# A gated delta-rule attention block: outputs and gates turned to time on the partitions

## The chip, the cores and the metric

The kernel runs on one core of one Trainium2 chip. The metric is device time of one execution in microseconds, lower is better. Times of a kernel are medians of several executions.

## What is computed

Three blocks in a row on an input of 4 x 512 tokens by 512: a feed-forward block whose weights are splines of control points, an attention block, and the feed-forward block again. The change touches the attention block alone. There, for each of 16 key heads (two value heads each) and each of 4 sequences:

```python
q, k, v, z = split(x @ W_qkvz)            # z gates the output
q, k, v = silu(causal_conv4(q, k, v))
q, k = rms_norm(q) / D, rms_norm(k) / sqrt(D)
S = S * exp(g_t)                          # per token t, per value head
delta = (v_t - k_t @ S) * beta_t
S = S + outer(k_t, delta)
o_t = q_t @ S
out = silu(z) * (rms_norm(o) * norm_w)    # norm over the 128 columns of a head
y += out @ W_out                          # sum over all heads
```

## The kernel before

**Phases.** The spline weights and the first feed-forward block take the start, then a norm phase, then `attn_phase`, then the second feed-forward block. `attn_phase` works through 64 units: a unit is one key head with its R = 2 value heads, for one sequence of S = 512 tokens, cut in CH = 4 chunks of P = 128. Unit j belongs to key head j // 4. Five engine programs (`pe_pass`, `act_pass`, `dve_pass`, `pool_pass`, `sp_pass`) are written out by hand in one order each, and wait for one another by counted semaphores. In slot j an engine handles the recurrence of unit j (`has_delta`), prepares unit j + 1 (`has_prep`: projections, convolutions, norms, the decay matrices), and finishes the output of unit j - 1 (`behind`).

**The inverse.** The first part of a slot inverts a 512-token set of unit-triangular 128 x 128 blocks by doubling, in level steps s = 2 to 13; step s works on value head g = s % 2. PE issues prod (four f16 matmuls into `psP`), DVE masks the result into `pm` (L2033), PE issues inv (eight f16 matmuls, L1657 and L1659, into `psT[g]`), ScalarE copies it out (`copy_t`, L1850). Steps 0 and 1 are `level_0` of either head; that of head 1 stands at the end of the slot before. Other work is hung on the steps: on PE `fill[s]` stands between prod(s) and inv(s); on DVE `steps[s]` stands behind the mask of step s and ahead of the mask of step s + 1; on ScalarE `steps[s]` stands behind the copy of inv(s).

**The chunks.** Then four chunks of the recurrence follow, with the rest of the projections in `gap`, and at the end `s_o` says that both heads' outputs are in PSUM, in `psO` (banks that `psT[1]` and `psP` use as well). POOL's copy of `dcy` (L2147) waits for `s_o` of the unit before and so opens the next slot.

**The output.** Values stand with the 128 columns of a head on the partitions and time along the free side. `squares` (ScalarE) squares `psO` into `osq`, DVE multiplies `psO` by `norm_w` and the silu of z (L2074, `d_gate`), `gated` rounds it to `gt_hi`, POOL takes the rest as `gt_lo` (`low_outputs`). `out_sums` on PE turns the squares into sums per token by 8 f32 matmuls of one column (16 passes), `out_scale` on POOL makes the factor `fr`. `out_product(i)` multiplies one head's chunk by `wo_hi`, `wo_lo` (three f32r matmuls of 512 columns into `out_bank`, which is `psM`), and `out_add` (L2007) multiplies by `fr` and adds into `resid`: eight products and eight additions a unit, in steps 5 to 12. The projection of z is 24 matmuls of 512 columns, with W as the stationary side. POOL also splits the weights of the next key head (`split_part`, `split_wo`) and masks the gates (`mask_g`).

Of the kernel before, what the change touches and what calls it, by code (L numbers as in the profile page):

```python
# [30 lines left out]
P = 128  # L31
# [4 lines left out]
D = 128  # L36
# [1221 lines left out]
WPROD = R * CH  # L1258
# [3 lines left out]
def attn_phase(nc, w_qkvz, conv_w, norm_w, w_out, cst_in, cst16_in, resid, x_hi, x_lo, gate_dram, decay_dram, y_dram):  # L1262
# [7 lines left out]
    with ExitStack() as ctx:  # L1270
# [3 lines left out]
        def sem(name):  # L1274
# [20 lines left out]
        cv_z = sb("cv_z", [P, R, S])  # L1295
# [158 lines left out]
        def pe_pass(pe):  # L1454
# [5 lines left out]
            for j, has_delta, has_prep, behind, ends in slots():  # L1460
                par = j % 2

                def bank_free(u, j):
# [5 lines left out]
                    if u == Z0_U:  # L1469
                        wait(pe, "d_conv", 4 * j + 1 if has_prep else 4 * j - 1)  # L1470
                        wait(pe, "d_sso", j)
# [30 lines left out]
                def out_product(i, of):  # L1502

                    h, c = i // CH, i % CH
                    wait(pe, "p_gt", R * of + h + 1)
                    if of % B == 0:
                        wait(pe, "p_wo", R * (of // B + 1))
                    if i > 0:
                        wait(pe, "d_y", WPROD * of + i)
                    else:  # L1510
                        wait(pe, "d_aqk", R * (j + 1))
                    out = out_bank[:]
                    mm(out, ch(gt_hi[:, h], c), wo_hi[:, h, :], True, False)
                    mm(out, ch(gt_hi[:, h], c), wo_lo[:, h, :], False, False)
                    own["s_w"].up(mm(out, ch(gt_lo[:, h], c), wo_hi[:, h, :], False, True))
# [52 lines left out]
                def out_sums(of):  # L1568

                    wait(pe, "a_sqo", R * (of + 1))  # L1570
                    if of == UNITS - 1:
                        wait(pe, "d_z", 2 * UNITS)
                    else:
                        wait(pe, "d_conv", 4 * j + 1 if has_prep else 4 * j - 1)
                    for i in range(R * CH):
                        last = mm(psA[0][:, i:i + 1], ch(osq[:, i // CH], i % CH), ones[:, 0:1])
                    own["s_sso"].up(last)

# [17 lines left out]
                gap = {g: [] for g in range(3 * CH)}  # L1596
                if behind:
                    fill[2].append(lambda: out_sums(j - 1))
                if has_prep:
                    fill[3].append(parts(Q_U, 7, 12))  # L1600
                if has_delta:
                    fill[4].append(parts(Z0_U, 0, 5))
                    fill[5].append(parts(Z0_U, 5, 6))
                    fill[6].append(parts(Z0_U, 7, 8))
                    fill[7].append(parts(Z0_U, 9, 10))
                    for k in range(5):
                        fill[8 + k].append(parts(Z1_U, 2 * k, 2 * k + 1))
                if behind:
                    for i in range(WPROD):
                        fill[5 + i].append(lambda i=i: out_product(i, j - 1))  # L1610
                if has_delta:
                    fill[5].append(parts(Z0_U, 6, 7))
                    fill[6].append(parts(Z0_U, 8, 9))
                    fill[7].append(parts(Z0_U, 10, 12))
                    for k in range(5):
                        fill[8 + k].append(parts(Z1_U, 2 * k + 1, 2 * k + 2))
                    fill[13].append(parts(Z1_U, 10, 12))
                if has_prep:
                    fill[13].append(turn_k)
# [87 lines left out]
                for c in range(CH):  # L1707
                    if has_delta:
# [3 lines left out]
                        else:  # L1712
# [6 lines left out]
                            for h in range(R):  # L1719
                                mm(ch(psO[h], c), state[:, h, :], ch(qg[:, h], c - 1), True, False)  # L1720
# [11 lines left out]
                    if has_delta:  # L1732
# [6 lines left out]
                        for h in range(R):  # L1739
                            last = mm(ch(psO[h], c), delta[:, h, :], ch(aqk[:, h], c), c == 0, True)  # L1740
# [10 lines left out]
                if ends:  # L1751
                    out_sums(j)
                    for i in range(WPROD):
                        out_product(i, j)
# [3 lines left out]
        def act_pass(act):  # L1758
            own = counters("a_")
            A = nc.scalar.activation  # L1760
            for j, has_delta, has_prep, behind, ends in slots():
# [90 lines left out]
                def squares(h):  # L1852
                    wait(act, "s_o", j + 1)
                    if h < R - 1:
# [11 lines left out]
                if behind:  # L1866
                    steps[2].append(lambda: gated(j - 1, 1))
                if has_prep:
                    steps[3].append(lambda: tap(Q_U))
                    steps[4].append(lambda: tanh(K_U))  # L1870
                    steps[7].append(lambda: tanh(Q_U))
                if has_delta:
                    steps[8].append(lambda: tanh_z(Z0_U))
                if has_prep:
                    steps[13].append(square_k)
# [47 lines left out]
                if has_delta:  # L1923
                    for h in reversed(range(R)):
                        squares(h)
                    gated(j, 0)
# [3 lines left out]
                if ends:  # L1930
                    gated(j, 1)
            finish(act, own)

        def dve_pass(dve):
# [8 lines left out]
            for j, has_delta, has_prep, behind, ends in slots():  # L1943
# [21 lines left out]
                def silu_z(u):  # L1965
                    wait(dve, "a_thz", 2 * j + u - 3)
                    wait(dve, "p_gt", R * j)
# [24 lines left out]
                def out_sums(i):  # L1992

                    wait(dve, "s_sso", i + 1)
# [364 lines left out]
```

How the kernel before makes its waits and increments, by code:

```python
            @block.gpsimd  # L380
            def _(pool):
                nc.gpsimd.memset(f32(st_g[:]), 0.0).then_inc(zeroed, 1)
                nc.gpsimd.memset(f32(st_b[:]), 0.0).then_inc(zeroed, 1)
                pool.dma_start(wts[:, 0:2 * GSUM], gsum_in).then_inc(sums_in, 16)
                pool.dma_start(groups(wts, S_FD, 4 * P), dsum_in.rearrange("p (g n) -> p g n", g=4)).then_inc(sums_in, 16)
                for u in range(UNITS + 4):
                    pool.wait_ge(hi_done, u + 1)
                    nc.gpsimd.tensor_tensor(weights(u, False), quarters(merged[:, u % 2, :]), f32(weights(u, True)), ALU.subtract).then_inc(lo_done, 1)
                pool.wait_ge(lo_done, UNITS + 4)
                pool.wait_ge(sums_in, 32)
# [1 line left out]
            @block.vector  # L392
# [4 lines left out]
                def chain(ins):  # L397
                    count[0] += 1
                    ins.then_inc(link, 1)
                    dve.wait_ge(link, count[0])
# [24 lines left out]
                    V.tensor_scalar(d3, c3, 0.5 * step ** 3, None, ALU.mult)  # L425
                    chain(V.tensor_scalar(d1, c1, 0.5 * step, None, ALU.mult))
                    if reach:
                        chain(V.scalar_tensor_tensor(d1, d3, float(reach), d1, ALU.mult, ALU.add))
                dve.wait_ge(tap_g_in, 32)
                cubics(tap_g, phi_g, d_g, NG, 0)
                dve.wait_ge(zeroed, 1)
# [30 lines left out]
                for u in range(UNITS + 4):  # L463
                    if u == 0:
                        dve.wait_ge(eval_in, 32)
                    if u == UNITS:
```

## Time and profile before

| | us |
|---|---|
| median of 3 runs (3988.17 to 3993.54) | 3991.61 |
| the profiled execution | 3988.65 |
| its span, first to last instruction | 3986.9 |
| PE matmul busy / weight loads busy | 3711.7 (93%) / 2984.8 (75%) |
| DVE / ScalarE (ACT) / POOL busy | 2447.1 (61%) / 1986.3 (50%) / 2344.9 (59%) |
| mean granted TensorE clock | 0.963 of 2.4 GHz |

Matmuls are pipelined: a duration reaches beyond the start of the next, so the distance between starts tells what one costs. A row of the timeline is start in us, duration in us, engine, line, operation, output <- inputs, shape, count; in brackets the idle time of the engine before it and what ended it. The f32 matmuls appear as two passes each. Units are counted from 0; unit j is the slot that POOL's copy of `dcy` opens for the (j + 1)th time.

### The profile page before, as it was taken

To read this page: it belongs to the slowest core of one execution; us is meant where nothing else is said; L and a number is where in the kernel's file an instruction comes from. 1 tells how busy PE (TensorE), PEld (TensorE's weight loads), DVE (VectorE), ACT (ScalarE), POOL (GpSimd) and SP (SyncE) were. 2 spreads that over 40 slices of the span, in tenths; PEclk is the share of its full clock that TensorE was granted. 3 is DMA by queue.
4 is the path that set the end of the run, shared out by engine and by line. 5 is a ranking of instruction groups with operands and counts; after the bars stand their busy time and mean duration, and the time that the engine had idled before them with its cause. 6 is when DMAs were issued, how large, how long until landed. Compare 5 with 4: busy or idle time off the path is not lost. (4 is left out here: it accounts for less than half of the span.)

```text
span 3986.9 us, 74528 instructions
## 1 busy us (share of the span) xinstructions
PE 3711.7 (93%) x28324; PEld 2984.8 (75%) x28324; DVE 2447.1 (61%) x4347; ACT 1986.3 (50%) x4272; POOL 2344.9 (59%) x2805
## 2 busy tenths in 40 slices
PE   5995699999999999999999999999999999998798
PEld 4884477777777777777777777777777777776587
DVE  4654366666666666666666666666666666664464
ACT  3432355555555555555555555555555555553243
POOL 2102567676766666676676767676767676763110
PEclk8997799999999999999999999999999999998899
DMA  4333100000000000000000000000000000001521
GB/s 165 97 33 67 50 22 23 23 23 22 23 22 23 22 23 22 23 22 23 22 23 22 23 23 23 22 23 22 23 22 23 19 22 22 25 16 36 175 54 33
DMA packets 142384, 140.32 MB, mean 35 GB/s; under 512 B 84176, under 2 KB 115152, under 8 KB 140880
## 3 DMA queue, kind: packets, MB, share of 16 engines
q1 hardware_dynamic: 136992, 120.16, 10.6%
q0 software_dynamic: 4464, 14.36, 1.0%
q8 instruction: 230, 3.77, 0.4%
q14 instruction: 122, 1.00, 0.1%
q10 hardware_dynamic: 576, 1.03, 0.1%
HBM read 109.11 MB, written 26.21 MB: 34 GB/s over the span
## 5 line engine op out<-in xcount | busy, mean ns | idle before, releaser
L1850 ACT ACTIVATE at_t<-at_inv 128x512 f16<-128x512 f32 x768 | 459.0, 598 | 783.0 <-PE at_inv L1659 783.0
L1458 PE MATMUL at_proj<-x_hi,at_w_hi 128*128 128x512 f32 x1536 | 669.4, 436 | 15.7 <-POOL at_w_lo L2103 15.7
L1458 PE MATMUL at_proj<-x_lo,at_w_hi 128*128 128x512 f32 x1536 | 663.4, 432 | 0.0
L1458 PE MATMUL at_proj<-x_hi,at_w_lo 128*128 128x512 f32 x1536 | 651.9, 424 | 0.0
L2033 DVE TENSOR_TENSOR at_pm<-at_prod,at_cst 128x512 f16<-128x512 f32 x768 | 529.6, 690 | 158.3 <-PE at_prod L1458 143.7
L2007 DVE SCALAR_TENSOR_TENSOR resid<-at_misc,at_fr,resid 128x512 f32<-128x512 f32 x512 | 383.3, 749 | 137.3 <-PE at_misc L1458 134.1
L1458 PE MATMUL at_prod<-at_t,at_nlhi 128*128 128x128 f16 x3584 | 377.5, 223 | 0.9 <-DVE at_pm L2040 0.9
L1657 PEld LDWEIGHTS at_inv<-at_pm,at_t 128*128 128x128 f16 x3072 | 214.0, 101 | 218.7 <-DVE at_pm L2033 139.0
L1458 PEld LDWEIGHTS at_proj<-x_hi,at_w_hi 128*128 128x128 f32 x1536 | 299.5, 195 | 55.3 <-issue 15.9
L1458 PEld LDWEIGHTS at_proj<-x_hi,at_w_lo 128*128 128x128 f32 x1536 | 301.8, 196 | 43.1
L1458 PEld LDWEIGHTS at_proj<-x_lo,at_w_hi 128*128 128x128 f32 x1536 | 303.6, 198 | 34.0
L1657 PE MATMUL at_inv<-at_pm,at_t 128*128 128x64 f16 x3072 | 298.6, 198 | 11.4 <-DVE at_pm L2033 3.8
L2181 POOL TENSOR_TENSOR at_gt_lo<-at_cst,at_gates 128x512 fp32r<-128x512 f32 x256 | 261.9, 1045 | 77.0 <-PE at_misc L1458 77.0
L1954 DVE SCALAR_TENSOR_TENSOR at_cv_v<-at_proj,at_cw,at_cv_v 128x511 f32<-128x511 f32 (+2 forms) x384 | 287.5, 749 | 15.5 <-ACT at_cv_v L1776 2.0
L1659 PE MATMUL at_inv<-at_t,at_pm 128*128 128x64 f16 x3072 | 292.1, 196 | 0.0
L1458 PEld LDWEIGHTS at_prod<-at_t,at_nlhi 128*128 128x128 f16 x3584 | 240.6, 100 | 19.5 <-issue 18.5
L2054 DVE SCALAR_TENSOR_TENSOR at_t<-at_t,at_dcy,at_inv 128x128 f32<-128x128 f32 x256 | 77.6, 345 | 286.1 <-PE at_inv L1458 277.8
L889 PE MATMUL f_ring<-f_x_hi,ffn_w 128*128 128x512 f32 x640 | 247.2, 401 | 3.9 <-DVE f_x_lo L815 2.9
L1899 ACT ACTIVATE at_t<-at_inv 128x256 f32<-128x256 f32 x256 | 98.5, 385 | 303.5 <-PE at_inv L1716 273.5
L1910 ACT ACTIVATE at_t<-at_inv,at_gates 128x128 f32<-128x128 f32 x512 | 160.0, 364 | 175.3 <-PE at_inv L1458 175.3
L1458 PE MATMUL at_misc<-at_wo_hi,at_gt_hi 128*128 128x512 f32 x512 | 232.3, 454 | 10.5 <-DVE resid L2007 9.1
L1659 PEld LDWEIGHTS at_inv<-at_t,at_pm 128*128 128x128 f16 x3072 | 218.6, 100 | 0.0
(282 smaller groups left out, 9512.3 us busy)
## 6 DMA issues: line engine op xcount, KB each, us to landing
at_gb<-decays SPq DMA_DIRECT2D x64, 512.0 KB, 3.7
at_e<-w_qkvz SPq DMA_DIRECT2D x32, 512.0 KB, 3.7
ffn_weights<-ffn_w SPq DMA_DIRECT2D x1, 11776.0 KB, 36.8
ffn_w<-ffn_weights POOLq DMA_DIRECT2D x4, 2688.0 KB, 23.5
at_gb<-w_qkvz SPq DMA_DIRECT2D x16, 512.0 KB, 3.6
at_gb<-w_out SPq DMA_DIRECT2D x16, 512.0 KB, 3.5
f_xnext<-x_in SPq DMA_DIRECT2D x4, 1024.0 KB, 5.2
f_xres<-x_res SPq DMA_DIRECT2D x4, 1024.0 KB, 5.2
```

What stands on the lines that cost most here:

```text
L889: return nc.tensor.matmul(out, lhsT, rhs, start=start, stop=stop)
L1458: return nc.tensor.matmul(out, lhsT, rhs, start=start, stop=stop)
L1657: nc.tensor.matmul(half_of(ch(psT[g], c), level, 0), ch(t16[:, g, 1], c), half_of(ch(pm[:, g], c), level, 0), start=False, stop=True, skip ...
L1659: last = nc.tensor.matmul(half_of(ch(psT[g], CH + c), level, 1), ch(pm[:, g], c), half_of(ch(t16[:, g, 1], c), level, 1), start=False, sto ...
L1850: own["a_t"].up(A(grown(t16[:, s % R].rearrange("p a t -> p (a t)"), s // R), grown(psT[s % R], s // R), ACT.Copy))
L1899: own["a_v"].up(A(vp, psV, ACT.Copy))
L1910: own["a_d"].up(A(delta[:, h, :], ch(psY, h), ACT.Copy, scale=gcur[:, 2, at + c, h:h + 1]))
L1954: ins = V.scalar_tensor_tensor(out[:, s:S], unit_bank[u][:, 0:S - s], cw[(j + 1) // B % 2][:, u, 3 - s:4 - s], out[:, s:S], ALU.mult, ALU.add)
L2007: own["d_y"].up(V.scalar_tensor_tensor(row, out_bank[:], fr[:, h, c:c + 1], row, ALU.mult, ALU.add))
L2033: own["d_p"].up(V.tensor_tensor(pm[:, g].rearrange("p (c t) -> p c t", c=CH), psP[:].rearrange("p (c t) -> p c t", c=CH), mask.unsqueeze(1 ...
L2054: ins = V.scalar_tensor_tensor(state[:, h, :], state[:, h, :], dcy[:, h, c:c + 1], ch(psU, h), ALU.mult, ALU.add)
L2181: last = G.tensor_tensor(gm[:, k], incl.unsqueeze(1).to_broadcast([P, CH, P]), new_gates[:, g, at:at + CH, h:h + 1].to_broadcast([P, CH, P ...
```

## The change

The outputs are held with time on the partitions. The operands of the `psO` products are swapped, so that `psO` is tokens by columns. z is projected with x as the stationary side and both heads' 256 columns of W moving (`gate_part`, 48 f32r matmuls a unit). ScalarE's squares add up per token by themselves (`accum_out`, four of 128 columns a head), and `out_sums` is gone from PE and DVE. POOL makes the factor first and multiplies the gated outputs by it (`scale_gated`); then PE turns them by transposes (`turn_gated`), ScalarE rounds them out of PSUM (`gated`), DVE takes the rest (`low`), and `out_product(c)` adds both heads of a chunk in one accumulator: six matmuls each, four products and four plain additions. `norm_w` goes into W_out. Some tasks stand in other steps: taps of K's convolution on DVE are spread, `turn_k` and `square_k` come a step earlier, POOL's splits of weights move behind `mask_g(1)`.

```diff
-WPROD = R * CH
+WPROD = CH
@@ pe_pass
+                def gate_part(u, first, end):
...
+                        last = mm(unit_bank[u][:, c * R * D:(c + 1) * R * D], xs[:, hb, tok:tok + P], w[:, hb, 4 * D:6 * D],
+                                  k % (3 * HB) == 0, k % (3 * HB) == 3 * HB - 1)
+                def turn_gated(h, of):
+                    wait(pe, "p_gt", R * of + h + 1)
+                    if h == 0:
+                        wait(pe, "d_aqk", R * (j + 1))
+                    else:
+                        wait(pe, "d_lo", R * of + h)
+                    for c in range(CH):
+                        last = nc.tensor.transpose(ch(psM, c), gated_of(h)[:, c, :], ident)
+                    own["s_gtr"].up(last)
+                def out_product(c, of):
...
+                    if c > 0:
+                        wait(pe, "d_y", WPROD * of + c)
+                    else:
+                        wait(pe, "d_lo", R * (of + 1))
+                    for h in range(R):
+                        mm(out, ch(gt_hi[:, h], c), wo_hi[:, h, :], h == 0, False)
+                        mm(out, ch(gt_hi[:, h], c), wo_lo[:, h, :], False, False)
+                        last = mm(out, ch(gt_lo[:, h], c), wo_hi[:, h, :], False, h == R - 1)
-                def out_sums(of):
...
-                        last = mm(psA[0][:, i:i + 1], ch(osq[:, i // CH], i % CH), ones[:, 0:1])
+                if has_prep:
+                    fill[2].append(parts(Q_U, 7, 9))
+                    fill[3].append(parts(Q_U, 9, 12))
+                if has_delta:
+                    fill[4].append(gates_in(Z0_U, 0, 8))
+                    fill[5].append(gates_in(Z0_U, 8, 16))
+                    fill[6].append(gates_in(Z0_U, 16, 24))
                 if behind:
+                    for h in range(R):
+                        fill[4 + h].append(lambda h=h: turn_gated(h, j - 1))
+                    for c in range(WPROD):
+                        fill[7 + c].append(lambda c=c: out_product(c, j - 1))
+                if has_delta:
+                    fill[8].append(gates_in(Z1_U, 0, 4))
+                    fill[9].append(gates_in(Z1_U, 4, 8))
+                    fill[10].append(gates_in(Z1_U, 8, 12))
+                    fill[11].append(gates_in(Z1_U, 12, 20))
+                    fill[12].append(gates_in(Z1_U, 20, 24))
+                    fill[12].append(turn_k)
...
-                                mm(ch(psO[h], c), state[:, h, :], ch(qg[:, h], c - 1), True, False)
+                                mm(ch(psO[h], c), ch(qg[:, h], c - 1), state[:, h, :], True, False)
...
-                            last = mm(ch(psO[h], c), delta[:, h, :], ch(aqk[:, h], c), c == 0, True)
+                            last = mm(ch(psO[h], c), ch(aqk[:, h], c), delta[:, h, :], c == 0, True)
@@ act_pass
                 def squares(h):
...
-                    own["a_sqo"].up(A(osq[:, h, :], psO[h], ACT.Square))
+                    for c in range(CH):
+                        last = A(osq[:, h, c * P:(c + 1) * P], ch(psO[h], c), ACT.Square, scale=2 * D ** -0.5, accum_out=sso[:, h, c:c + 1])
                 def gated(of, h):
-                    wait(act, "d_gate", R * of + h + 1)
-                    own["a_gt"].up(A(gt_hi[:, h, :], cv_z[:, h, :], ACT.Copy))
+                    wait(act, "s_gtr", R * of + h + 1)
+                    own["a_gt"].up(A(gt_hi[:, h, :], out_bank[:], ACT.Copy))
...
+                if behind:
+                    for h in range(R):
+                        steps[4 + h].append(lambda h=h: gated(j - 1, h))
@@ dve_pass
+                def low(h, of):
+                    wait(dve, "a_gt", R * of + h + 1)
...
+                    own["d_lo"].up(V.tensor_tensor(gt_lo[:, h, :], out_bank[:], gt_hi[:, h, :], ALU.subtract))
+                def out_add(c, of):
+                    wait(dve, "s_w", WPROD * of + c + 1)
                     row = resid[:, of % B * CH + c, :]
-                    own["d_y"].up(V.scalar_tensor_tensor(row, out_bank[:], fr[:, h, c:c + 1], row, ALU.mult, ALU.add))
+                    own["d_y"].up(V.tensor_tensor(row, out_bank[:], row, ALU.add))
...
+                if has_prep and has_delta:
+                    steps[2].append(lambda: conv(K_U, (3,)))
...
+                if behind:
+                    steps[4].append(lambda: low(0, j - 1))
+                if has_prep:
                     steps[4].append(lambda: conv(Q_U, (1,)))
...
+                    steps[5].append(lambda: low(1, j - 1))
...
+                    for c in range(WPROD):
+                        steps[7 + c].append(lambda c=c: out_add(c, j - 1))
...
-                            conv(K_U, (1, 2, 3), j + 1)
+                            conv(K_U, (1,), j + 1)
...
-                        own["d_gate"].up(V.scalar_tensor_tensor(cv_z[:, h, :], psO[h], nw[:, 0:1], cv_z[:, h, :], ALU.mult, ALU.mult))
+                        own["d_gate"].up(V.tensor_tensor(gated_of(h), psO[h].rearrange("p (c v) -> p c v", c=CH), gated_of(h), ALU.mult))
+                if has_prep and j + 2 < UNITS:
+                    conv(K_U, (2,), j + 1)
@@ pool_pass
                 def out_scale(of):
-                    wait(pool, "d_sso", of + 1)
-                    wait(pool, "d_y", WPROD * of)
+                    wait(pool, "a_sqo", R * (of + 1))
+                    chain(G.tensor_tensor(sso[:], sso[:], qs2[:, of % 2, :].unsqueeze(1).to_broadcast([P, R, CH]), ALU.mult))
...
+                def scale_gated(of, h):
+                    wait(pool, "d_gate", R * of + h + 1)
+                    own["p_gt"].up(G.tensor_tensor(gated_of(h), gated_of(h), fr[:, h, :].unsqueeze(2).to_broadcast([P, CH, D]), ALU.mult))
...
-                    if j % B == 0:
-                        split_wo(kh)
-                    if j % B == B - 1:
-                        split_part(kh + 1, 2)
                     mask_g(1)
                     for h in range(R):
                         wait(pool, "a_ex", R * j + h + 1)
                         own["p_ex"].up(G.affine_select(e2[:, h, :], e2[:, h, :], [[0, CH], [1, P]], ALU.is_ge, 0.0, base=0, channel_multiplier=-1))
+                        if j % B == 0:
+                            split_wo(kh, h)
+                        if has_delta and j % B == B - 1:
+                            split_part(kh + 1, 2, range(h * HB // 2, (h + 1) * HB // 2))
```

## Rows read from the trace of the kernel before

**Rows 1.** POOL copy that opens each unit, by its line, and in order of time:

```profile
L2147 POOL COPY at_dcy<-at_gb x64: 193/194/196, 468.7 to 3620.5; 128x8 f32<-128x8 f32 x64
...
1768.27 0.20 POOL L2147 COPY at_dcy<-at_gb 128x8 f32<-128x8 f32 x1 [4.73 <-PE at_prod L1458]
...
1816.95 0.19 POOL L2147 COPY at_dcy<-at_gb 128x8 f32<-128x8 f32 x1 [4.72 <-PE at_prod L1458]
```

**Rows 2.** Timeline of unit 26, its marks on PE, and DVE's gate product:

```profile
1768.92 0.74 DVE L2074 SCALAR_TENSOR_TENSOR at_cv_z<-at_inv,at_nw,at_cv_z 128x512 f32<-128x512 f32 x1
...
1770.47 0.38 PE L1458 MATMUL at_inv<-at_pm,at_cst 128*128 128x512 f16 x1 [0.63 <-ACT at_aqk L1856]
...
1771.13 1.90 PE L1458 MATMUL at_proj<-at_cst,at_aqk 128*128 128x1 f32 x16
...
1776.27 0.20 PE L1657 MATMUL at_inv<-at_pm,at_t 128*128 128x64 f16 x1
...
1792.77 0.20 PE L1657 MATMUL at_inv<-at_pm,at_t 128*128 128x64 f16 x1
```

**Rows 3.** Timeline of unit 26, three engines, steps 3 to 6:

```profile
1774.57 0.20 PE L1657 MATMUL at_inv<-at_pm,at_t 128*128 128x64 f16 x1
...
1774.82 0.38 PE L1458 MATMUL at_prod<-at_t,at_nlhi 128*128 128x128 f16 x4
...
1775.02 0.60 ACT L1850 ACTIVATE at_t<-at_inv 128x512 f16<-128x512 f32 x1 [0.58 <-PE at_inv L1659]
...
1775.24 0.69 DVE L2033 TENSOR_TENSOR at_pm<-at_prod,at_cst 128x512 f16<-128x512 f32 x1 [0.22 <-PE at_prod L1458]
...
1775.51 0.68 ACT L1776 ACTIVATE at_cv_q<-at_proj,at_cw 128x512 f32<-128x512 f32 x1
...
1776.23 0.75 DVE L1954 SCALAR_TENSOR_TENSOR at_cv_q<-at_proj,at_cw,at_cv_q 128x511 f32<-128x511 f32 x1 [0.29 <-ACT at_cv_q L1776]
...
1777.01 0.69 DVE L2033 TENSOR_TENSOR at_pm<-at_prod,at_cst 128x512 f16<-128x512 f32 x1
...
1779.42 0.69 DVE L2033 TENSOR_TENSOR at_pm<-at_prod,at_cst 128x512 f16<-128x512 f32 x1
...
1780.03 0.74 DVE L2007 SCALAR_TENSOR_TENSOR resid<-at_misc,at_fr,resid 128x512 f32<-128x512 f32 x1
...
1780.17 0.20 PE L1657 MATMUL at_inv<-at_pm,at_t 128*128 128x64 f16 x1
```

**Rows 4.** Timeline of unit 26, a product and the additions around it:

```profile
1777.98 0.75 DVE L2007 SCALAR_TENSOR_TENSOR resid<-at_misc,at_fr,resid 128x512 f32<-128x512 f32 x1 [0.28 <-PE at_misc L1458]
...
1778.88 0.47 PE L1458 MATMUL at_misc<-at_wo_hi,at_gt_hi 128*128 128x512 f32 x1
...
1779.43 0.40 PE L1458 MATMUL at_misc<-at_wo_hi,at_gt_lo 128*128 128x512 f32 x1
```

**Rows 5.** Timeline of unit 27, accumulating squares, and POOL's scale chain:

```profile
1822.00 0.25 POOL L2122 TENSOR_SCALAR at_sso<-at_sso 128x8 f32<-128x8 f32 x1 [1.11 <-DVE at_sso L1995]
...
1824.24 1.29 POOL L2129 TENSOR_TENSOR at_gt_lo<-at_cv_z,at_gt_hi 128x512 fp32r<-128x512 f32 x1
...
1843.90 0.27 ACT L1812 ACTIVATE at_kn<-at_misc 128x128 f32<-128x128 f32 x1
...
1844.15 0.28 ACT L1812 ACTIVATE at_kn<-at_misc 128x128 f32<-128x128 f32 x1
```

**Rows 6.** What PE waited for (us in total, times, longest); the wait for kn:

```profile
PE at_misc L1458 <- POOL at_gt_lo L2181: 37.6, 32, 3.6
...
1848.06 0.66 PE L1539 MATMUL at_misc<-at_cst,at_kn 128*128 128x128 f32 x4 [0.30 <-ACT at_kn L1819]
```

**Rows 7.** Stretches (us, busy, then PEclk, DMA share, GB/s); inv(4) of unit 27:

```profile
1822.00:1823.00 1.00, 1.00 (x9) 0.90 (x7) 0.89 (x2) 0.81 (x2) 0.92 (x2) 0.50 0.00 0
...
1826.48 0.20 PE L1657 MATMUL at_inv<-at_pm,at_t 128*128 128x64 f16 x1
```

More of the change, by code:

```diff
@@ L1500, in proj @@
                     proj_part(u, 3 * hbs[0], 3 * hbs[-1] + 3, i)
-                def out_product(i, of):
-                    h, c = i // CH, i % CH
-                    wait(pe, "p_gt", R * of + h + 1)
-                    if of % B == 0:
+                def gate_part(u, first, end):
+                    if first == 0:
+                        if j % B == 0:
+                            wait(pe, "p_z", j // B + 1)
+                        bank_free(u, j)
+                    for k in range(first, end):
+                        c, hb = k // (3 * HB), k % (3 * HB) // 3
+                        tok = j % B * S + (2 * (u - Z0_U) + c) * P
+                        w, xs = ((w_hi, x_hi), (w_hi, x_lo), (w_lo, x_hi))[k % 3]
+                        last = mm(unit_bank[u][:, c * R * D:(c + 1) * R * D], xs[:, hb, tok:tok + P], w[:, hb, 4 * D:6 * D],
+                                  k % (3 * HB) == 0, k % (3 * HB) == 3 * HB - 1)
+                    if end == 6 * HB:
+                        own["s_z"].up(last)
@@ L1596, in pe_pass, with gates_in @@
                 gap = {g: [] for g in range(3 * CH)}
-                if behind:
-                    fill[2].append(lambda: out_sums(j - 1))
-                if has_prep:
[L1600 to L1619, printed above, removed]
+                def gates_in(u, first, end):
+                    return lambda: gate_part(u, first, end)
+                if has_prep:
[5 more added lines that the diff above has]
+                    fill[6].append(gates_in(Z0_U, 16, 24))
+                if behind:
+                    for h in range(R):
[8 more added lines that the diff above has]
+                    fill[12].append(gates_in(Z1_U, 20, 24))
+                if has_prep:
+                    fill[12].append(turn_k)
                     fill[14].append(parts(V0_U, 0, 4))
@@ L1751, in pe_pass @@
                 if ends:
-                    out_sums(j)
-                    for i in range(WPROD):
-                        out_product(i, j)
+                    for h in range(R):
+                        turn_gated(h, j)
+                    for c in range(WPROD):
+                        out_product(c, j)
             finish(pe, own)
@@ L1930, in act_pass @@
                 if ends:
-                    gated(j, 1)
+                    for h in range(R):
+                        gated(j, h)
             finish(act, own)
@@ L1966, in silu_z @@
                     wait(dve, "a_thz", 2 * j + u - 3)
-                    wait(dve, "p_gt", R * j)
+                    wait(dve, "s_gtr", R * j)
                     own["d_z"].up(V.scalar_tensor_tensor(cv_z[:, u - Z0_U, :], th[:, u % 2, :], 1.0, unit_bank[u][:], ALU.add, ALU.mult))
@@ L2088, in chain, with split_part @@
                 pool.wait_ge(link.sem, link.n)
-            def split_part(kh, part):
+            def split_part(kh, part, hbs=range(HB)):
                 wait(pool, ("l_kq", "l_v", "l_z")[part], 16 * (kh + 1))
```

100 lines of the change are left out of this document (42 added, 58 removed).

## The prediction, made before the changed kernel was run

> **What bounds the kernel now.** I read the busy slices first, then the starts of one POOL instruction that opens every unit, then one unit engine by engine in order of time. The attention phase is 64 units alike; POOL's copy of dcy opens each, 63 intervals between its first and last start give 3151.8/63 = 50.03 us a unit, and the unit I use as measure takes 48.68 [rows 1]. Within a unit no single engine is full: each level step s of the inverse is a loop through three engines. PE issues prod(s), DVE masks it into pm, PE issues inv(s) behind whatever filler the step has, ScalarE copies the result. PE runs this in order, so a step costs the larger of its PE work and of the round trip. The marks that I count from (time 0 is the opening copy, 1768.27) are level_0 at 2.20, the one-column sums at 2.86, inv(4) at 8.00 and inv(13), the last level, at 24.50 [rows 2].
>
> **The handoffs, and the floor of a step.** In [rows 3]: prod to pm 0.42; pm to inv 0.75; inv to ScalarE's copy 0.45; that copy to ScalarE's next instruction 0.49; end of a ScalarE instruction to DVE 0.04; a mask to DVE's next instruction 0.61; a conv tap that is followed by a wait on itself to the next mask 0.78. So inv(s) can't come before 0.42 + 0.75 after prod(s), and with the 0.25 of inv a step has a floor of 1.42. On PE a step costs 0.20 for prod, 0.25 for inv (1774.57 to 1774.82), and its filler: 0.235 for a 128x512 matmul, plus 0.08 for the first of a series (0.55 for the two from 1778.88 to 1779.43) [rows 4]. The sixteen one-column passes of f32 take 1.90, 0.12 each, which is the pace of a weight load [rows 2].
>
> **Part by part, the head of the unit.** Removed: sixteen one-column passes (out_sums), which hold PE for 1.90 while pm(2) is long ready [rows 2]. Added in their place on ScalarE: eight squares of 128 columns with accumulation; the same form comes every 0.25 [rows 5], so 1.0 for one head against 0.60. DVE's K convolution is split so that only one tap stands before the gate product; today three do, and the gate begins 0.65 after time 0 [rows 2]. Now: squares(1) 0 to 1.0, gate(0) 0 to 0.7, gate(1) 1.05 to 1.75, squares(0) 1.0 to 2.0, level_0 at 2.1, prod(2) 2.55, pm(2) 2.97, inv(2) 3.7. Tap 3 of K and the two qk products now queue on DVE ahead of pm(3), which starts at about 4.9: inv(3) at 5.65. POOL's qg ends at 2.2; the scale chain takes 2.24 today and has one more small operation, 2.55, then the two multiplications by the factor at 1.3: done at 6.1 and 7.4 [rows 5]. Step 4: prod 0.2, eight half-width gate matmuls, four transposes at 0.12. For the half-width f32r matmul the trace has no row: below stands the 0.12 of a weight load, above 0.12 + half of 0.235 = 0.235 if nothing overlaps. I take 0.13, since a 512-wide one plainly hides its load. So inv(4) = 5.9 + 0.2 + 0.08 + 1.04 + 0.48 = 7.7, against 8.00. The sums are gone but only 0.3 is left of them.
>
> The Trainium skill (TensorE: Matmul & The Clock Gate, "The mechanism") says that a weight load overlaps with matmuls in flight only when the row group differs. Here all 128 rows are used, and yet the 512-wide matmuls follow each other in 0.235, which is less than load and matmul together [rows 2, 4]; the trace speaks against it. By the rule 48 gate matmuls would cost twice their present share; that is a rival below.
>
> **Steps 5 and 6, the point on which I decide.** DVE's tasks of step s stand between pm(s) and pm(s+1); ScalarE's tasks of step s stand after the copy of inv(s). The change puts gated(h) on ScalarE and low(h) on DVE into the same step 4 + h, and low(h) waits for gated(h). So pm(5) waits for low(0), that for gated(0), that for the copy of inv(4). Queued behind low(0) on DVE are Q's tap and pm(5); behind pm(5) stands all of PE. The chain: inv(4) to copy 0.45, to gated 0.49, to low 0.62 + 0.04, to the Q tap 0.61, to pm(5) 0.78, to inv(5) 0.75: 3.7. PE has only 0.25 + 0.2 + 1.12 + 0.48 = 2.05 to do meanwhile (1.57 in the next step). The same once more for low(1): inv(5) at 11.4, inv(6) at 15.1. inv(6) stood at 11.90 before (1780.17) [rows 3].
>
> **Steps 7 to 10.** One accumulator takes six matmuls per chunk: four additions instead of eight, but each product waits for the addition before it, with nothing of PE's between except prod and inv. Last matmul to addition 0.60, addition to next product 0.90 [rows 4]; the new addition is a plain one, 0.06 shorter, as the mask's 0.69 against 0.75. From the end of one product to the end of the next: 0.37 + 0.84 + 0.08 + 6 x 0.235 = 2.70. The first ends at 15.1 + 0.25 + 0.2 + 0.08 + 1.41 = 17.1, the fourth at 25.2. Then Z1's four halves (0.6) put inv(10) at 25.8; inv(11) 1.57 later, inv(12) 1.53, inv(13) the floor 1.42: 30.3. Before: 24.50. That is +5.8. DVE's saved additions (four of 0.75) buy nothing: it isn't DVE's load but its order that counts.
>
> **The rest.** turn_k comes a step earlier, which takes away PE's wait for kn after newton, 0.30 and the handoff behind it [rows 6]: -0.4. POOL's weight splits move behind a_ex, so the wait for gm goes, 37.6 us in 32 units, 0.59 a unit [rows 6]; but they now stand ahead of the diagonal selects, for which ScalarE's copies to f16 wait. Between 0 and -0.6 I take -0.3. Swapped operands of the psO products: 128 columns on both sides, nothing. norm_w moved into W_out: once in four units on POOL, under PE's work; if that cover goes, POOL's 1.3 on that unit, 0.3 a unit. The gated outputs' scaling on POOL replaces a subtraction of the same size. **The clock.** It falls to half (0.50) in one stretch of unit 27 right after the idle time and the one-column passes, and puts inv(4) at 9.53 instead of 8.00, 1.5 us [rows 7]. Over all units this is 50.03 - 48.68 - 0.59 = 0.8 a unit. The cause there goes, but the waits of 1.7 and 2.2 us in steps 5 and 6 make a stretch just as thin. I keep 0.8, with 0 and 1.6 as bounds.
>
> **The sum.** 5.8 - 0.4 - 0.3 = 5.1 a unit, by 63 units that have a unit behind them: +321. The drain behind the last unit (eight products before, then four longer ones behind the longer chain of gated and low) I leave at nothing, an estimate good to some 5 us. The profiled execution took 3988.65 (span 3986.9 and 1.75 around it): 4310. The median shown is 3 above it: 4313.
>
> **Rivals.**
> 1. Forecast, low(h) holds up the masks and each product waits for the addition: 4313, chance 0.70.
> 2. The same, but the clock is at half once or twice in every unit: +0.8 to +1.6 by 63, 4363 to 4410. For it: the idle in steps 5 and 6 exceeds today's 0.63. Against: some full-width work lies between. 0.10.
> 3. low(h) isn't late (ScalarE gets to gated before its copy, or the order is not what I read): steps 5 and 6 cost PE's 2.05 and 1.57, 3.84 less a unit: 4071. Against it stands the written order of the queues. 0.10.
> 4. Faster: PE bound by its own work, as in rival 3, and moreover the additions are covered (0.76 + 0.16 + 0.16 less) and the clock never falls (0.8 less): 5.1 - 3.84 - 1.08 - 0.8 = -0.6 a unit, 3953 in all. It decides from where PE's waits in steps 4 to 10 stay under 0.6 us a unit in sum; PE's removed 1.9 us speak for it. 0.06.
> 5. Weight loads not hidden behind half-width matmuls: 0.235 each instead of 0.13. In steps 5 and 6 that is covered, in the others it costs about 2.5 a unit: 4470. 0.04.
>
> **Range and chances.** 8 in 10: below, the clock's 0.8 gone and POOL's full 0.6 gained (-70) with some 20 for handoffs that I rounded up; above, case 2. 4220 to 4410; rivals 3 to 5 (0.20) lie outside. 0.2% (8 us) is about what a measurement of this kernel tells from no change. Faster by more: 0.06; within: 0.01; slower: 0.93.
>
> **What would show it.** Right: DVE's mask of step 5 starts some 2.8 us after inv(4), directly behind a Q tap that follows low(0), and PE waits for at_pm about 1.7 and 2.2 us in steps 5 and 6; the first matmuls of products 2 to 4 wait for resid; units take about 55 us. Wrong: masks of steps 5 and 6 within 0.5 us of prod; half-width matmuls 0.2 us apart; a granted clock of 1.00 throughout or 0.5 for more than one stretch a unit; squares later than 2.2 us after the unit's opening; PE waiting for p_gt before the transposes.

## The result and the profile after

The changed kernel takes 4247.18 us (median of 4 runs, 4243.03 to 4261.48) against 3992.19 for the kernel before on the same chip: 1.0647 times as long, interval 1.062 to 1.0674. The prediction was 4313, 4220 to 4410. The profiled execution took 4261.48, the slowest of the four, and its span is 4259.7; counts and waits below are of that one.

| per unit, us | before | after |
|---|---|---|
| mean of the 63 periods | 50.03 | 54.32 |
| shortest unit, full clock all through | 48.64 | 52.84 |
| PE busy in one such unit (windows of 49 and 53 us) | 48.00 | 46.93 |
| stretches of half clock in 63 units | 36 | 49 |

The page of after (busy time and share by engine), and the group of POOL's opening copy:

```profile
PE 3677.4 (86%) x29348; PEld 3085.0 (72%) x29348; DVE 2345.2 (55%) x4155; ACT 2046.1 (48%) x5168; POOL 2394.0 (56%) x2931
```

```profile
L2178 POOL COPY at_dcy<-at_gb x64: 192/194/197, 468.3 to 3890.3; 128x8 f32<-128x8 f32 x64
```

PE and DVE do less work than before and the kernel is slower: the opening copies [rows 1] are now (3890.3 - 468.3)/63 = 54.32 us apart. What PE waited for, in us, times and longest:

```profile
PE at_inv L1675 <- DVE at_pm L2057: 274.7, 322, 2.1
PE at_misc L1528 <- DVE at_gt_lo L2020: 50.0, 64, 1.6
PE at_inv L1462 <- ACT at_aqk L1877: 44.7, 63, 2.3
...
PE at_inv L1462 <- ACT at_t L1923: 32.8, 17, 2.3
...
PE at_misc L1462 <- DVE resid L2026: 11.8, 36, 0.8
```

PE waited 274.7 us for the masks; the same wait in before was 3.8. The wait for gm [rows 6] is gone, and one of the same size has come (L1923, 32.8 in 17 times). Line numbers are those of after: L1675 inv, L1528 the transposes of the gated output, L2057 the mask, L2020 `low`, L1883 `gated`, L2026 the addition, L1869 the copy of the inverse.

**Unit 26, opened at 1876.04.** The timeline of PE, ScalarE and DVE in steps 4 to 6 (start, duration, engine, line; in brackets the idle time ahead and what ended it), where [rows 3] stood before:

```profile
1883.73 0.19 PE L1675 MATMUL at_inv<-at_pm,at_t 128*128 128x64 f16 x1
...
1884.16 0.60 ACT L1869 ACTIVATE at_t<-at_inv 128x512 f16<-128x512 f32 x1 [0.72 <-PE at_inv L1677]
1884.66 0.59 ACT L1883 ACTIVATE at_gt_hi<-at_misc 128x512 fp32r<-128x512 f32 x1
...
1884.95 0.28 PE L1462 MATMUL at_proj<-at_w_lo,x_hi 128*128 128x256 f32 x1
1885.07 0.28 PE L1462 MATMUL at_proj<-at_w_hi,x_hi 128*128 128x256 f32 x1
...
1885.28 0.69 DVE L2020 TENSOR_TENSOR at_gt_lo<-at_misc,at_gt_hi 128x512 fp32r<-128x512 f32 x1 [2.10 <-ACT at_gt_hi L1883]
1885.89 0.74 DVE L1978 SCALAR_TENSOR_TENSOR at_cv_q<-at_proj,at_cw,at_cv_q 128x511 f32<-128x511 f32 x1
1886.12 0.63 PE L1528 MATMUL at_misc<-at_cst,at_cv_z 128*128 128x128 f32 x4 [0.77 <-DVE at_gt_lo L2020]
1886.66 0.69 DVE L2057 TENSOR_TENSOR at_pm<-at_prod,at_cst 128x512 f16<-128x512 f32 x1
...
1887.41 0.20 PE L1675 MATMUL at_inv<-at_pm,at_t 128*128 128x64 f16 x1 [0.67 <-DVE at_pm L2057]
...
1891.11 0.20 PE L1675 MATMUL at_inv<-at_pm,at_t 128*128 128x64 f16 x1 [2.06 <-DVE at_pm L2057]
```

From inv(4) the chain runs as predicted: copy after 0.43, `gated` 0.50, `low` 0.62 with DVE idle for 2.10 ahead of it, the Q tap 0.61, the mask 0.77, inv(5) 0.75: 3.68 in all. Step 6 repeats it, 3.70. The two half-width rows show their pitch, 0.12. The transposes of the second head wait as well, 0.77 for `low(0)` at 1886.12, since they write the bank that it reads; in this order the mask ends later still, so that wait adds nothing.

### The profile page after: what moved, and what is told of

Its sections match the earlier page's. It is cut to its first block and busy times, and to the rows that moved or that the text cites. A ratio compares the mean times of both kernels' runs of the same rounds, so it can differ in the third digit from the quotient of the medians.

```text
span 4259.7 us, 76953 instructions
## 1 busy us (share of the span) xinstructions
PE 3677.4 (86%) x29348; PEld 3085.0 (72%) x29348; DVE 2345.2 (55%) x4155; ACT 2046.1 (48%) x5168; POOL 2394.0 (56%) x2931
## 3 DMA queue, kind: packets, MB, share of 16 engines
q14 instruction: 128, 1.05, 0.1%
## 5 line engine op out<-in xcount | busy, mean ns | idle before, releaser
L1869 ACT ACTIVATE at_t<-at_inv 128x512 f16<-128x512 f32 x768 | 460.8, 600 | 990.9 <-PE at_inv L1677 990.9
L2057 DVE TENSOR_TENSOR at_pm<-at_prod,at_cst 128x512 f16<-128x512 f32 x768 | 530.0, 690 | 183.9 <-PE at_prod L1462 167.8
L1675 PE MATMUL at_inv<-at_pm,at_t 128*128 128x64 f16 x3072 | 299.0, 198 | 274.8 <-DVE at_pm L2057 274.7
L1675 PEld LDWEIGHTS at_inv<-at_pm,at_t 128*128 128x128 f16 x3072 | 211.3, 99 | 412.2 <-DVE at_pm L2057 369.4
L1462 PE MATMUL at_proj<-x_hi,at_w_hi 128*128 128x512 f32 x1024 | 438.5, 428 | 16.0 <-POOL at_w_lo L2131 16.0
L1462 PE MATMUL at_proj<-x_lo,at_w_hi 128*128 128x512 f32 x1024 | 426.8, 417 | 0.0
L1462 PE MATMUL at_proj<-x_hi,at_w_lo 128*128 128x512 f32 x1024 | 417.2, 407 | 0.0
L2026 DVE TENSOR_TENSOR resid<-at_misc,resid 128x512 f32<-128x512 f32 x256 | 177.0, 692 | 277.5 <-PE at_misc L1462 277.5
L1462 PE MATMUL at_proj<-at_w_lo,x_hi 128*128 128x256 f32 x1024 | 298.4, 291 | 0.0
L1462 PE MATMUL at_proj<-at_w_hi,x_hi 128*128 128x256 f32 x1024 | 298.0, 291 | 0.0
L1462 PE MATMUL at_proj<-at_w_hi,x_lo 128*128 128x256 f32 x1024 | 292.7, 286 | 0.0
L1462 PE MATMUL at_misc<-at_wo_hi,at_gt_hi 128*128 128x512 f32 x512 | 250.4, 489 | 13.9 <-DVE resid L2026 11.8
L2218 POOL TENSOR_SCALAR at_rr<-at_ss 128x4 f32<-128x4 f32 x64 | 14.9, 233 | 401.1 <-ACT at_kn L1831 324.7
L1462 PEld LDWEIGHTS at_proj<-x_hi,at_w_hi 128*128 128x128 f32 x1024 | 195.5, 191 | 39.8 <-issue 16.2
L1462 PE MATMUL at_misc<-at_wo_lo,at_gt_hi 128*128 128x512 f32 x512 | 223.5, 436 | 0.0
```

Source lines behind the costliest of these rows:

```text
L1462: return nc.tensor.matmul(out, lhsT, rhs, start=start, stop=stop)
L1675: nc.tensor.matmul(half_of(ch(psT[g], c), level, 0), ch(t16[:, g, 1], c), half_of(ch(pm[:, g], c), level, 0), start=False, stop=True, skip ...
L1869: own["a_t"].up(A(grown(t16[:, s % R].rearrange("p a t -> p (a t)"), s // R), grown(psT[s % R], s // R), ACT.Copy))
L2026: own["d_y"].up(V.tensor_tensor(row, out_bank[:], row, ALU.add))
L2057: own["d_p"].up(V.tensor_tensor(pm[:, g].rearrange("p (c t) -> p c t", c=CH), psP[:].rearrange("p (c t) -> p c t", c=CH), mask.unsqueeze(1 ...
L2218: chain(G.tensor_scalar(rr[:, 0:CH], ss[:, 0:CH], EPS_RMS, None, ALU.add))
```

## Experiments

Each kernel is the changed one with the edit shown, but for one that starts from the kernel before. Marks are us from the unit's opening, in the shortest unit of each kernel at full clock, the first and the last period left out; half clock is the number of stretches, of which nine of the 16 of e7_best last twice as long as all others.

| kernel | inv(4) | inv(5) | inv(6) | inv(10) | inv(13) | shortest unit | mean unit | half clock |
|---|---|---|---|---|---|---|---|---|
| before | 7.99 | 9.67 | 11.90 | 19.31 | 24.47 | 48.64 | 50.03 | 36 |
| after | 7.69 | 11.38 | 15.07 | 24.79 | 29.10 | 52.84 | 54.32 | 49 |
| e1_low_later | 7.68 | 10.54 | 12.02 | 22.15 | 26.46 | 50.18 | 51.07 | 15 |
| e4_spread | 7.68 | 9.16 | 11.36 | 20.32 | 26.31 | 50.04 | 51.09 | 22 |
| e2_gates_first | 7.68 | 11.36 | 15.06 | 24.32 | 28.70 | 52.43 | 53.76 | 37 |
| e8_taps | 7.26 | 10.95 | 14.64 | 24.38 | 28.69 | 52.43 | 53.62 | 38 |
| e6_wo_early | 7.68 | 11.37 | 15.06 | 24.79 | 29.10 | 52.83 | 53.70 | 33 |
| e7_best | 6.79 | 8.54 | 10.52 | 19.47 | 25.30 | 48.75 | 49.94 | 16 |
| e10_best | 6.79 | 8.27 | 10.24 | 19.24 | 24.64 | 48.05 | 48.04 | 1 |

**e1_low_later: `low(h)` one step later in DVE's queue.**

```diff
-                if behind:
-                    steps[4].append(lambda: low(0, j - 1))
...
-                    steps[5].append(lambda: low(1, j - 1))
+                    for h in range(R):
+                        steps[5 + h].append(lambda h=h: low(h, j - 1))
```

> The changed kernel with one move: on DVE low(h) stands one step later (steps 5 and 6 instead of 4 and 5), behind the mask of that step. Theory A (low(h), waiting for gated(h) of the same step, holds up the masks): inv(4) to inv(5) falls from 3.69 to about 2.9 us (PE's transposes of head 1 still wait for low(0)), inv(5) to inv(6) from 3.69 to about 1.5, and the first product then waits some 0.5 for low(1); in sum -2.5 us a unit, about 4090 us in all. Rival B (the time is set by the longer chain transposes, gated, low, products, wherever low stands): what steps 5 and 6 gain comes back as a wait of the first product, inv(7) stays near 17.0 us after the unit's opening, 4235 to 4250 us.

Measured 4054.67 us, 1.0149 (1.013 to 1.0167). The timeline of DVE in its unit 26, opened at 1796.17:

```profile
1804.58 0.69 DVE L2056 TENSOR_TENSOR at_pm<-at_prod,at_cst 128x512 f16<-128x512 f32 x1 [0.23 <-PE at_prod L1462]
1805.41 0.69 DVE L2020 TENSOR_TENSOR at_gt_lo<-at_misc,at_gt_hi 128x512 fp32r<-128x512 f32 x1
1806.02 0.74 DVE L1978 SCALAR_TENSOR_TENSOR at_cv_q<-at_proj,at_cw,at_cv_q 128x510 f32<-128x510 f32 x1
1807.45 0.69 DVE L2056 TENSOR_TENSOR at_pm<-at_prod,at_cst 128x512 f16<-128x512 f32 x1 [0.69 <-PE at_prod L1462]
```

The mask of step 5 waits for nothing but its product, and `low` follows it with 0.14 of idle time between. One place in one queue is worth 192 us of the 255 that the change cost. Of the 208 us between the two profiled executions 168 are the shorter chain (2.66 a unit, 52.84 to 50.18); the other 40 are the clock, whose half stretches fall from 49 to 15.

**e4_spread: transposes and `gated` in steps 4 and 6, `low` in 5 and 7, each product behind the gates' matmuls and in a step of its own.**

```diff
-                        fill[4 + h].append(lambda h=h: turn_gated(h, j - 1))
+                        fill[4 + 2 * h].append(lambda h=h: turn_gated(h, j - 1))
...
-                        fill[7 + c].append(lambda c=c: out_product(c, j - 1))
+                        fill[8 + c].append(lambda c=c: out_product(c, j - 1))
...
-                        steps[4 + h].append(lambda h=h: gated(j - 1, h))
+                        steps[4 + 2 * h].append(lambda h=h: gated(j - 1, h))
```

> The changed kernel with the output work spread: transposes in steps 4 and 6, gated in 4 and 6, low in 5 and 7, products and additions in 8 to 11, each behind the gate matmuls of its step, of which eight fill step 7. Theory A (order, not the amount of work, costs the time): inv(13) comes at about 25.6 us after the unit's opening instead of 29.1 and at 24.5 in the kernel before; with the half clock as often as now about 4025 us, without it about 3970. Rival B (the additional matmuls and transposes themselves cost it): above 4150 us.

Measured 4057.59, 1.0156 (1.0141 to 1.0172): slower than expected and no better than e1_low_later. inv(6) comes 0.66 earlier than there, but the products and their additions, a step later, give back all but 0.15 by inv(13). The second head's transposes no longer wait for `low(0)` (a wait of 50.2 us in 64 times in e1_low_later, of 1.6 in one here). But the gates' matmuls are used up by step 11: in a unit at full clock PE now waits 0.48 for the mask of step 12, where e1_low_later has no wait (135.0 us for masks in all, against 104.2), and the turning of K waits for the last addition (25.0 us in all). The delay was moved along the unit, not removed.

**e2_gates_first: in steps 8 to 10 the gate's matmuls ahead of the product.**

```diff
-                if behind:
-                    for h in range(R):
-                        fill[4 + h].append(lambda h=h: turn_gated(h, j - 1))
-                    for c in range(WPROD):
-                        fill[7 + c].append(lambda c=c: out_product(c, j - 1))
                 if has_delta:
...
+                if behind:
+                    for h in range(R):
+                        fill[4 + h].append(lambda h=h: turn_gated(h, j - 1))
+                    for c in range(WPROD):
+                        fill[7 + c].append(lambda c=c: out_product(c, j - 1))
```

> The changed kernel with the gate matmuls of steps 8 to 10 issued ahead of that step's output product instead of behind it. The trace of the changed kernel shows only one wait of a product for an addition, 0.47 us ahead of the second; the others find theirs done. Theory A (only this wait is exposed): -0.47 us a unit, about 4217 us. Rival B (every product waits for its addition, as the prediction had it at 2.70 us from product to product): -1.1 us a unit, about 4178 us. Rival C: the half clock falls in these steps and takes the gain, no change.

Measured 4226.22, 1.0584 (1.0568 to 1.06); the shortest unit is 0.41 shorter. A unit of the changed kernel thus has one exposed wait for an addition, not three; the whole fell by 21 us. The rows of after say why, PE and DVE around the first three products, where [rows 4] stood before:

```profile
1891.55 0.48 PE L1462 MATMUL at_misc<-at_wo_hi,at_gt_hi 128*128 128x512 f32 x1
...
1892.79 0.40 PE L1462 MATMUL at_misc<-at_wo_hi,at_gt_lo 128*128 128x512 f32 x1
...
1893.23 0.69 DVE L2026 TENSOR_TENSOR resid<-at_misc,resid 128x512 f32<-128x512 f32 x1 [0.76 <-PE at_misc L1462]
...
1893.97 0.50 PE L1462 MATMUL at_misc<-at_wo_hi,at_gt_hi 128*128 128x512 f32 x1 [0.31 <-DVE resid L2026]
...
1895.24 0.39 PE L1462 MATMUL at_misc<-at_wo_hi,at_gt_lo 128*128 128x512 f32 x1
1895.46 0.28 PE L1462 MATMUL at_proj<-at_w_hi,x_hi 128*128 128x256 f32 x1
...
1895.66 0.69 DVE L2026 TENSOR_TENSOR resid<-at_misc,resid 128x512 f32<-128x512 f32 x1 [1.15 <-PE at_misc L1462]
...
1896.41 0.49 PE L1462 MATMUL at_misc<-at_wo_hi,at_gt_hi 128*128 128x512 f32 x1
```

Between the second and the third product PE has four half-width gate matmuls, which just cover the addition: the third product starts 0.75 after it (1895.66 to 1896.41), much as the second does (0.74, 1893.23 to 1893.97), but PE is busy until then. Only the second product (1893.97) waits.

**e8_taps: K's third tap on DVE directly behind the second, before the unit opens.**

```diff
-                if has_prep and has_delta:
-                    steps[2].append(lambda: conv(K_U, (3,)))
...
-                    conv(K_U, (2,), j + 1)
+                    conv(K_U, (2, 3), j + 1)
```

> The changed kernel with K's third tap taken from step 2 on DVE to directly behind the second, ahead of the first mask. Theory A (the tap and qk ahead of the mask of step 3 cost the 0.62 us that PE waits there): inv(3) moves from 5.78 to about 5.4 us after the unit's opening, inv(4) from 7.69 to 7.3, and so -0.4 us a unit, about 4222 us. Rival B: the first mask is now late by as much, no change within 8 us.

Measured 4212.53, 1.0548 (1.053 to 1.0565). inv(3) falls from 5.78 to 5.35 after the opening and the shortest unit by nearly the same, 0.41: the tap stood in the chain of masks, as the prediction had it.

**e6_wo_early: the split of the output weights on POOL ahead of its wait for the key sums.** Every fourth unit of the changed kernel (j a multiple of 4) is longer, 56.65 on the mean against some 53.7 for the others. The timeline of POOL, ScalarE and PE in unit 28 of after, near its end:

```profile
2025.66 1.58 POOL L2139 TENSOR_SCALAR at_gb<-at_gb,at_nw 128x512 f32<-128x512 f32 x1
...
2030.19 1.57 POOL L2139 TENSOR_SCALAR at_gb<-at_gb,at_nw 128x512 f32<-128x512 f32 x1
...
2033.77 0.65 POOL L2239 TENSOR_SCALAR_AFFINE_SELECT at_nl<-at_nl 128x512 f32<-128x512 f32 x1
...
2034.44 0.63 ACT L1861 ACTIVATE at_nlhi<-at_nl 128x512 f16<-128x512 f32 x1 [2.69 <-POOL at_nl L2239]
...
2036.71 0.37 ACT L1923 ACTIVATE at_t<-at_inv 128x256 f32<-128x256 f32 x1
...
2037.13 0.71 PE L1462 MATMUL at_inv<-at_t,at_sq 128*128 128x128 f32 x4 [2.00 <-ACT at_t L1923]
```

Both heads' splits (from 2025.66 to 2033.8) stand ahead of the selects of `nl`; ScalarE's f16 copies wait for those, and the copy that PE needs is queued behind them.

```diff
+                    if j % B == 0:
+                        for h in range(R):
+                            split_wo(kh, h)
                     wait(pool, "a_ssk", j + 1)
...
-                        if j % B == 0:
-                            split_wo(kh, h)
```

> The changed kernel with POOL's splitting of W_out moved from between the selects of the decay matrices to the idle stretch ahead of the factor for k. Theory A (in one unit of four the split keeps ScalarE's f16 copies, and behind them its copy of v' and PE, waiting 2.2 us): these units fall from 55.1 to about 53.3 us, 16 units, -25 to -35 us, about 4217 us. Rival B: the split now holds up the factor for k by as much, no change within 8 us.

Measured 4222.12, 1.0575 (1.0559 to 1.059). The wait of L1923 is gone and every fourth unit takes 54.98, 1.67 less; at full clock it is 53.97 against 55.11, 1.14 less. Not the full 2.2, since the split now delays the key factor, for which PE waits 18.1 us in 16 units.

**e9_half_width: the kernel before, its z projection in half-width matmuls.** This takes the price of the new width out of the change.

```diff
+                        if u >= Z0_U:
+                            half_s = S // 2
+                            for n in range(2):
+                                last = nc.tensor.matmul(unit_bank[u][:, n * half_s:(n + 1) * half_s], w[:, hb, UNIT_COL[u]:UNIT_COL[u] + D],
+                                                        xs[:, hb, tok + n * half_s:tok + (n + 1) * half_s],
...
```

> The kernel before with each of the 24 matmuls of the z projection split into two of 256 columns with a weight load each, nothing else. Theory A (load and matmul overlap, 0.118 us from start to start as in the trace of the changed kernel, 0.235 for 512 columns): nothing within 12 us of the kernel before. Rival B (the amount of weight loads costs, 0.235 each): +2.8 us a unit or some +180 us.

Measured 3992.48, 1.0001 (0.9992 to 1.001). Two rows of its timeline of PE:

```profile
1771.89 0.39 PE L1497 MATMUL at_proj<-x_hi,at_w_hi 128*128 128x256 f32 x2
1772.12 0.39 PE L1497 MATMUL at_proj<-x_lo,at_w_hi 128*128 128x256 f32 x2
```

Two half-width matmuls take 0.23, as one of 512 did [rows 4], though each brings its own weight load of 128 rows. Rival 5 falls. With it falls, for this kernel, the rule of the Trainium skill (TensorE: Matmul & The Clock Gate, "The mechanism") as the prediction quoted it, that a weight load overlaps only when the row group differs. The same section also lets a load run ahead when it goes to a background weight buffer; that would fit these rows, and no run here shows whether it is the reason.

**e7_best: the orders of e4_spread, e6_wo_early and e8_taps together, and PE's filler moved to where it waits.**

```diff
-                    fill[2].append(parts(Q_U, 7, 9))
-                    fill[3].append(parts(Q_U, 9, 12))
+                    fill[2].append(parts(Q_U, 10, 12))
...
+                    for s, a, b in ((2, 0, 4), (3, 4, 11), (4, 11, 15), (5, 15, 21), (6, 21, 24)):
+                        fill[s].append(gates_in(Z0_U, a, b))
...
-                    fill[14].append(parts(V0_U, 0, 4))
-                    fill[15] += [parts(V0_U, 4, 9), sums]
+                    fill[12] += [turn_k, parts(V0_U, 0, 2)]
+                    fill[13].append(parts(V0_U, 2, 5))
...
-                    proj_part(Q_U, 0, 7)
+                    proj_part(Q_U, 0, 10)
```

> The spread kernel (transposes and gated in steps 4 and 6, low in 5 and 7, products and additions in 8 to 11), W_out's splits moved to POOL's idle stretch, and PE's filler put where PE waits: ten Q matmuls instead of seven ahead of level_0, gate matmuls from step 2 on, five matmuls of V0 moved from step 15 into steps 12 and 13; on DVE both last taps of K directly behind the gate products. Theory A (what is left above PE's work is waits in steps with too little filler: 0.8 ahead of level_0, 0.5 and 0.6 in steps 2 and 3, 0.9 in step 13): inv(13) at about 24.4 us after the opening, units of 47 to 48 us, 3820 to 3880 us in all, under both kernels. Rival B: the moved matmuls are missed where they came from, units stay near 50 us, 4000 to 4050.

Measured 3982.41, 0.9974 (0.9964 to 0.9985): barely faster than before, and over 100 us short of what was expected. Three units in four take 48.77; every fourth takes 53.56. The reason, in PE's timeline of unit 28, and the clock behind it (stretch, its length, busy time and instruction count of PE, PEld, DVE, ACT and POOL, then PEclk, DMA share, GB/s):

```profile
1899.32 1.11 PE L1568 MATMUL at_misc<-at_cst,at_kn 128*128 128x128 f32 x4 [3.46 <-ACT at_kn L1834]
```

```profile
1899.00:1903.00 4.00, 3.68 (x14) 3.39 (x15) 0.00 (x0) 1.62 (x5) 2.46 (x5) 0.50 0.06 20
```

With PE ahead of where it was, POOL's whole split stands between it and the key factor: PE is idle for 3.46, then runs at 1.2 GHz. What cost some 1 us in e6_wo_early cost nearly 5 here.

**e10_best: that split in two halves, the key factor between them; two parts of V's projection ahead of the turning of K; Q's first tap a step earlier on ScalarE.**

```diff
-                        for h in range(R):
-                            split_wo(kh, h)
+                        split_wo(kh, 0)
...
+                        if j % B == 0 and h == 0:
+                            split_wo(kh, 1)
...
-                    fill[12] += [turn_k, parts(V0_U, 0, 2)]
+                    fill[12] += [parts(V0_U, 0, 2), turn_k]
...
-                    steps[3].append(lambda: tap(Q_U))
+                    steps[2 if has_delta else 3].append(lambda: tap(Q_U))
```

> Same work as e7_best, with two things moved: GpSimd's split of the output projection's weights is cut in two halves with the key factor's chain between them, so that the factor no longer stands behind the whole split in every fourth unit; and three filler matmul groups of V stand ahead of turn_k, where TensorE waits 0.57 us in e7_best. Theory A (in e7_best every fourth unit is 53.6 us against 48.8 because TensorE waits 3.6 us for the key factor behind that split, and the half clock follows from that wait): every fourth unit falls to 49 to 50.5 us, the others by 0 to 0.8 us, the half clock stretches to fewer than in e7_best, the whole to 3850 to 3920 us. Rival B (the long units come from the weight DMA or from ScalarE's copies, not from the factor's place on GpSimd): they stay at 53 us or above and the whole at 3960 us or above.

(The lines are against e7_best.) Measured 3859.02 us (3858.92 to 3862.51), 0.9674 (0.9658 to 0.969): faster than both kernels. Its page, its opening copies, two units of its windows, and what PE still waits for:

```profile
PE 3604.3 (93%) x29348; PEld 3007.1 (78%) x29348; DVE 2331.0 (60%) x4155; ACT 2037.5 (53%) x5168; POOL 2390.2 (62%) x2931
```

```profile
L2169 POOL COPY at_dcy<-at_gb x64: 191/193/193, 468.3 to 3494.8; 128x8 f32<-128x8 f32 x64
```

```profile
1812.00:1860.00 48.00, 46.70 (x419) 39.37 (x418) 30.90 (x54) 27.74 (x75) 38.28 (x45) 1.00 0.08 25
1860.00:1908.00 48.00, 46.79 (x420) 39.49 (x419) 30.39 (x54) 27.69 (x75) 31.11 (x39) 1.00 0.04 12
```

```profile
PE at_misc L1568 <- ACT at_kn L1834: 41.0, 63, 1.7
...
PE at_misc L1528 <- DVE at_gt_lo L2016: 28.0, 63, 1.6
```

Of the 63 periods 61 lie between 48.05 and 48.30 (the first and the last, with less to do, are shorter), one stretch of half clock is left, and theory A holds. Every fourth unit fell further than expected, to 48.17. Q's tap on ScalarE is a move that the expectation doesn't name, and its share in the 0.7 of the other units wasn't separated. Against before, a unit is 1.99 shorter: 0.6 in the shortest unit, the other 1.4 in what the mean had above it, PE's wait for gm and the half clock. Of the work that the change takes off PE, the two waits shown (41.0/63 and 28.0/63) still hide 1.1 a unit. How much of this the same care with the order would have given the kernel before wasn't tried.

## Why the prediction came out as it did

- **Direction and mechanism: right.** Rival 1, the forecast, came true: `low(h)`, waiting for `gated(h)`, holds up the mask of the next step. inv(4), inv(5), inv(6) were put at 7.7, 11.4 and 15.1 and came at 7.69, 11.38 and 15.07. e1_low_later undid that link alone and took back 192 of 255 us, so the cause is shown. Rivals 3 and 4 needed masks behind their products, which DVE's rows refute; rival 2 needed the half clock in every unit or twice, and it came 49 times in 63. The tap in front of the masks was placed rightly too (e8_taps). Of the three products that were to wait for an addition, one did.
- **Products, the term that was mis-sized.** The pitch from product to product was put at 2.70. It is 2.42 and 2.44 (1891.55, 1893.97, 1896.41). The step that failed is the way through the addition: 0.60 from the last matmul to it, and 0.90, less 0.06, from it to the next product. Those were read from rows in which neither engine waited for the other. The addition at 1780.03 stood on DVE behind the mask of 1779.42 [rows 3], and the product at 1778.88 behind other work of PE [rows 4]; neither row has idle time ahead. Where DVE was idle, the rows of after show 0.44 (1892.79 to 1893.23), and from there 0.74 to the product that waits (1893.97). That is 1.18 instead of 1.44, 0.26 less, which is the whole difference of the pitch.
- **Its filler.** "Nothing of PE's between except prod and inv" holds for the first pitch alone; the gate matmuls stand behind products 2 to 4. This did not spoil the sum: with four of them PE's work between two products is 1.05 by the prediction's figures, less than the 1.21 that it gave the addition, and rival 4 counts them (0.16 of wait left). With the shorter way they cover the addition.
- **What it made.** Three pitches are 0.8 of the 1.2 by which inv(13) came early, at 29.1 and not 30.3: +4.63 instead of +5.8. The rest is a half-width pitch of 0.118 instead of 0.13, and small roundings. This is most of the miss.
- **The rest of the unit.** -0.4 was predicted behind inv(13); (52.84 - 29.10) - (48.64 - 24.47) = -0.43.
- **POOL's splits.** Taken at -0.3, between 0 and -0.6. The wait for gm, 0.59, did go. But the risk named, the selects and ScalarE's f16 copies behind the splits, came in full: 2.2 us in every fourth unit, 0.56 a unit. Net 0: the upper bound. The term was bounded rightly and its middle taken without a reason; the length of the splits on POOL should have been laid against the time of the selects.
- **The clock.** 0.8 was kept. Units with a half stretch, set against full-clock units in the same place of their group of four, give 1.56 for each of the 36 stretches of before, 0.9 a unit (50.22 against 48.67 in the second of each group), and some 1.3 for each of the 49 of after, 1.0 a unit. The size nearly held, and the place moved: see below.
- **The sum.** 4.63 - 0.43 + 0 + 0.1 = 4.3, by 63 is 271; the profiled executions differ by 272.8, the medians by 255, since the one profiled after is the slowest of its four. Predicted was 321.

## What to carry to other kernels

Before moving a step onto two engines, write down for each in-order queue what stands behind the new wait: here a subtraction whose input came one step too late held up the mask behind it, and through it all of TensorE, and one step's difference in place was worth 4.5% of the kernel. Read a handoff between two engines only from rows in which the second engine was idle and says what ended its wait; the distance between two instructions that were both queued behind other work is no handoff, and here it made a pitch of 2.44 into 2.70. When a stage gets shorter, look again at the edits that cost nothing before: a split that cost 1 us with PE behind cost 5 with PE ahead.

## What the runs showed of the hardware

**The half clock came behind idle time, and mostly went with it.** In before all 36 stretches began 4.3 to 5.4 us after a unit's opening, behind the idle time and the one-column passes [rows 2, 7]. The changed kernel has none there, but 43 that begin 14.9 to 16.5 us in, behind the waits of steps 5 and 6. The windows of unit 27 of after, opened at 1928.88 (columns as above):

```profile
1936.00:1944.00 8.00, 4.50 (x53) 3.88 (x52) 4.20 (x8) 2.98 (x6) 5.77 (x6) 1.00 0.43 133
1944.00:1947.40 3.40, 3.40 (x19) 2.49 (x19) 1.24 (x2) 0.60 (x1) 3.32 (x4) 0.51 0.00 0
1947.40:1952.00 4.60, 4.30 (x40) 3.64 (x40) 2.67 (x4) 1.71 (x3) 4.60 (x5) 0.99 0.00 0
```

PE is busy 4.50 of 8 us at full clock, then runs 3.4 us at 1.2 GHz, though it now has all the work it can take. In e1_low_later this stretch is gone and 15 are left, 14 of them at the end of a fourth unit, behind the wait for ScalarE there; in e7_best they follow the wait for the key factor; in e10_best one is left. Removing a wait of 2 us therefore returned more than 2 us, which the expectation of e1_low_later left out: put at 4090, it came at 4055. Not every such wait is followed by a stretch: 18 units of after run at full clock all through, and why those wasn't found.

**Splitting a matmul in two by columns is free here.** 128x256 f32r matmuls follow each other in 0.118, 128x512 ones in 0.235, with a new weight load each; split so, the kernel before takes 3992.48 against 3992.08.
